# A three-stage decoder kernel: denominator products in rounded halves, table loads as steps of their own, the last feed-forward chunk stacked, and a new order of all steps

## Time and profile before

| | us |
|---|---|
| median of three runs | 876.79 |
| lowest and highest | 876.32, 876.93 |
| the profiled execution | 872.71 |
| its span, first to last instruction | 870.9 |
| a round of the loop | 49.9 |
| PE busy in the span | 824.3 (95%) |
| DVE busy | 698.4 (80%) |
| ACT busy | 587.0 (67%) |
| POOL busy | 262.5 (30%) |
| granted clock, mean | 0.999 |

### The profile page before, as it was taken

How to read it: one execution, slowest core, us unless ns; L and a number is a source line. 1 busy time by engine, 2 the same in 40 slices (tenths; PEclk the granted TensorE clock), 3 DMA queues, 4 the chain that set the end, 5 groups by cost and what they waited for, 6 DMA issues and landing times. The chain is left out here.

```text
span 870.9 us, 21260 instructions
## 1 busy us (share of the span) xinstructions
PE 824.3 (95%) x7296; PEld 699.3 (80%) x7296; DVE 698.4 (80%) x1673; ACT 587.0 (67%) x1527; POOL 262.5 (30%) x443
## 2 busy tenths in 40 slices
PE   9888999999899999999999999999999999998986
PEld 5667788888788888888888888888888888876764
DVE  6889789796979879797988979798897979785643
ACT  5465478785776777686776868676786768674632
POOL 0304223333323333332332233332232333222231
PEclk9999999999999999999999999999999999999999
DMA  8231201111020111111011111111111111101010
GB/s 292 78 101 36 64 14 43 50 50 56 36 62 16 42 48 48 54 41 61 13 41 60 36 54 48 54 36 34 44 39 51 48 54 37 56 2 44 13 55 7
DMA packets 31223, 44.03 MB, mean 51 GB/s; under 512 B 2512, under 2 KB 23120, under 8 KB 31184
## 3 DMA queue, kind: packets, MB, share of 16 engines
q1 hardware_dynamic: 27696, 32.94, 11.4%
q0 software_dynamic: 2048, 6.30, 2.4%
q10 hardware_dynamic: 1440, 4.28, 1.6%
HBM read 28.81 MB, written 14.70 MB: 50 GB/s over the span
## 5 line engine op out<-in xcount | busy, mean ns | idle before, releaser
L681 ACT ACTIVATE prob<-bank,b_folded 128x256 f32<-128x256 f32 x128 | 53.6, 470 | 97.8 <-PE bank L1125 96.8
L872 DVE TENSOR_TENSOR a_s<-bank,const 128x512 f32<-128x512 f32 x112 | 71.2, 682 | 47.4 <-PE bank L1229 26.5
L718 ACT ACTIVATE w_raw_or_stage_c<-bank,c_nmax 128x128 f32<-128x128 f32 x256 | 90.4, 402 | 15.3 <-DVE c_nmax L1038 15.3
L718 ACT ACTIVATION_READ_ACCUMULATOR w_raw_or_stage_c<-bank,c_nmax 128x1 f32 x256 | 62.1, 243 | 0.0
L785 DVE TENSOR_TENSOR b_s_lo<-prob,b_s_hi 128x512 fp32r<-128x512 f32 x64 | 45.3, 708 | 8.2 <-ACT b_s_hi L565 8.2
L443 POOL TENSOR_TENSOR f_rs<-f_mv,const 128x2 f32<-128x2 f32 x32 | 6.1, 191 | 147.5 <-DVE f_mv L794 147.5
L1038 DVE TENSOR_REDUCE c_nmax<-bank 128x4 f32<-128x512 f32 x64 | 40.5, 676 | 11.6 <-PE bank L1409 11.6
L1125 PE MATMUL bank<-b_s_hi,w_mlp_hi 128*128 128x256 f32 x256 | 45.1, 299 | 0.4 <-ACT prob L681 0.3
L1511 PE MATMUL bank<-ones_bf 128*128 128x512 bf16 x160 | 44.4, 396 | 1.0 <-POOL ones_bf L435 1.0
L1420 PE MATMUL bank<-const,w_raw_or_stage_c 128*128 128x128 f32 x256 | 39.6, 278 | 5.5 <-ACT w_raw_or_stage_c L718 4.9
L565 ACT ACTIVATE b_s_hi<-prob 128x512 fp32r<-128x512 f32 x64 | 41.1, 642 | 3.6 <-PE bank L1125 3.0
(11 more groups left out here) (257 smaller groups left out, 2683.7 us busy)
## 6 DMA issues: line engine op xcount, KB each, us to landing
token_rows<-norm_x_rms SPq DMA_DIRECT2D x16, 513.0 KB, 3.8
x_in<-in_x SPq DMA_DIRECT2D x16, 256.0 KB, 3.3
qc<-in_ctx SPq DMA_DIRECT2D x16, 256.0 KB, 2.7
b_f<-in_ctx_t SPq DMA_DIRECT2D x16, 256.0 KB, 3.0
x<-in_x SPq DMA_DIRECT2D x16, 256.0 KB, 2.7
out<-w_raw_or_stage_c SPq DMA_DIRECT2D x16, 256.0 KB, 2.2
w_raw_or_stage_c<-in_w ACTq DMA_DIRECT2D x4, 512.0 KB, 6.3
w_raw_or_stage_c<-in_w_gu ACTq DMA_DIRECT2D x4, 341.0 KB, 3.2
```

The lines of the kernel that those rows point to most:

```text
L681: act_in(prob[:, 2 * (j % 2) + n, :], b0[:, n * T:(n + 1) * T], ACT.Gelu, bias=b1p[:, f:f + 1]).then_inc(b_gelu.sem, 1)
L718: act_in(c_e[g % 2][:, j * R:(j + 1) * R], C_SCORES[g][:, j * R:(j + 1) * R], ACT.Exp, bias=c_nmax[:, n:n + 1], accum_out=c_den[:, head:he ...
L872: tt(heads(A_MASKED[t][n][:, :]), heads(A_SCORES[n][:, :]), tri.unsqueeze(1).broadcast_to([P, 4, P]), ALU.mult).then_inc(a_scput.sem, 1)
```

## The change

Denominator: `a_kq`'s product is split into a high part (new step `a_qhi`, ACT) and a low part (new step `a_qlo`, DVE) in the tiles of `a_tr`, and `a_den` makes four rounded products with the block matrix, which is now kept rounded (`head_block_r`), in place of two plain ones. The block matrix and the row of indices are loaded into a work tile and copied from there.

Last chunk: 682 features fill five chunks of 128 and 42 of the sixth (FL = 42). The 42 are now written three times: the last chunk of the gated values holds the high part, the low part's source and its copy beside each other (two more DVE operations in `c_gate_1`), W3's last chunk holds matching high and low rows, and `c_ff_1` needs one product for it in place of three. `c_gtlo_1` works on two chunks.

Tables: the preload of `a_qout` goes; three steps `b_set_ln`, `b_set_exp` and `b_set_gelu` load the three sets.

Order: all steps stand in a new order, and WEIGHTS_AT and WARM_AT are new (193 filler products in place of 146, besides the 14 at the start).

```diff
+FL = FF % P
+FLAT = FF - FL
...
-a_kout+ c_gu_1++ b_dtp+ b_rtp+ c_tanh_1++ c_gu_2++ b_sid+ b_fput+ b_dput+ b_rput+ b_fmean+ a_ktp+ c_gtlo_1++
-c_gtp_0++ c_gtp_1++ a_vput+ b_kept++ a_sput+ b_fd+ a_den+ c_hsc+ b_fnormed+ a_mask+ b_sexp+ a_dnear+ c_y++
-c_gthi_0++ a_kput+ c_ff_0++ c_gthi_1++ a_state+ a_dinv+ a_rstd+ c_ff_1++ b_hlo+ a_scput_0+ c_ht+ b_htp+
-a_scput_1+ a_scput_2+ a_scput_3+ a_score_0+ a_dput+ a_scput_4+ c_qk+ c_hput+ b_hhi+ b_gelu_0+ b_up_0+ b_fb2++
-a_scput_5+ a_score_1+ c_v+ a_scput_6+ a_scput_7+ a_att_0+ b_rstd+ b_up_1+ b_qb+ c_qkput+ b_glo_0+ a_mean
-a_att_1+ a_y+ b_glo_1+ b_ghi_0+ b_gelu_1+ b_ghi_1+ b_up_2+ a_ylo+ a_normed b_glo_2+ b_orstd++ c_rstd+ c_max_0+
-c_max_1+ b_down_0+ b_up_3+ c_score+ c_max_2+ a_proj+ b_down_1+ a_done+ b_mean c_etp_0+ c_rms1+ c_max_3+ b_glo_3+
-b_down_2+ c_etp_1+ c_vput+ c_etput_0+ b_normed b_down_3+ b_gelu_2+ a_yhi+ c_etput_1+ c_etp_2+ b_ghi_2+ b_gelu_3+
-b_o+ c_h2rms++ c_exp_0+ c_hx++ c_dinv+ c_pick+ c_etp_3+ c_exp_1+ c_etput_2+ b_ghi_3+ c_etput_3+ b_omean+ a_tlo
-c_exp_2+ c_exp_3+ a_tp c_o+ b_tanhk b_onormed+ b_done+ c_mean c_h2put+ c_dtp+ b_pnorm c_dbc+ c_normed c_h2lo+
-b_diff c_rscore a_thi b_frstd+ c_rank c_att+ c_dput+ c_sel b_vq b_v c_idxput c_put++ b_ratio c_keep+ c_gate_0+
-b_tanhq a_phi_q b_vput c_h2sq+ c_ob+ c_xo+ a_phi_k c_h2hi+ a_qout a_q b_log c_gate_1+ a_csum c_h2tp+ a_kq a_k
-c_gu_0+ c_sbc c_tanh_0+ a_val c_gtlo_0+ c_idx
+b_qb+ a_vput+ c_sbc+ b_set_ln b_sexp+ c_gthi_0++ b_orstd++ c_gu_0++ a_kput+ a_qlo+ a_qhi+ b_fput+ c_gtlo_1++
+b_fmean+ a_dnear+ c_idx+ c_gu_1++ a_sput+ a_mask+ c_gthi_1++ a_dput+ c_rstd+ c_y++ b_dtp+ c_hput+ b_fnormed+
+b_set_exp c_rms1+ a_scput_0+ a_scput_1+ b_rtp+ b_hlo+ c_gu_2++ a_scput_2+ a_scput_3+ b_sid+ a_ktp+ b_hhi+
+a_scput_4+ a_dinv+ b_glo_0+ a_scput_5+ a_scput_6+ c_hx++ c_h2rms++ a_scput_7+ b_gelu_0+ c_gtp_0++ a_mean a_y+
+b_ghi_0+ b_fd+ b_gelu_1+ c_qkput+ c_pick+ a_ylo+ c_gtp_1++ b_glo_1+ a_den+ c_ff_0++ b_gelu_2+ a_normed b_glo_2+
+c_ht+ a_state+ c_ff_1++ b_frstd+ b_ghi_1+ c_max_0+ c_max_1+ a_score_0+ b_htp+ c_max_2+ c_vput+ c_qk+ a_yhi+
+a_done+ b_ghi_2+ b_up_0+ b_gelu_3+ c_exp_0+ b_mean c_put++ c_max_3+ b_glo_3+ c_exp_1+ a_score_1+ c_etput_0+
+b_normed c_v+ a_att_0+ b_up_1+ c_etput_1+ b_ghi_3+ b_fb2+ c_exp_2+ c_exp_3+ a_att_1+ b_o+ b_up_2+ b_down_0+
+c_dinv+ a_thi c_etput_2+ b_up_3+ c_dbc+ c_score+ a_proj+ c_etput_3+ c_ob+ b_down_1+ c_etp_0+ b_set_gelu++
+c_dput+ b_tanhk b_down_2+ b_omean+ c_etp_1+ b_kept+ b_down_3+ a_tlo c_etp_2+ c_o+ a_tp c_etp_3+ b_onormed+
+b_tanhq b_done+ c_dtp+ a_rstd c_h2put+ c_keep+ c_att+ c_h2sq+ c_xo+ c_mean a_qout b_pnorm c_normed c_rscore
+b_diff c_h2lo+ a_q c_rank c_sel b_vq a_phi_q c_idxput a_kout b_ratio c_h2hi+ b_vput c_h2tp+ b_log c_tanh_0+
+a_phi_k c_tanh_1+ a_k c_gate_0+ b_v a_csum a_val b_rstd a_kq c_gate_1+ b_dput b_rput c_gtlo_0+ c_hsc
...
-                if not first(b):
-                    nc.scalar.preload_act_table_set("natural_log_exp_and_others")
...
+            def a_qhi_(b):
+                act_e.wait_ge(*a_kq(b))
+                act_e.wait_ge(*a_qk(b))
+                act_e.wait_ge(*a_val(b))
+                copy(flat(a_tr[0][:, :, :]), a_e0[:, :], a_qhi)
+
+            def table(name):
+                def step(b):
+                    nc.scalar.preload_act_table_set(name)
+                return step
...
+                    if n == len(loads) - 1:
+                        last = [w[:, FFP // P - 1, :] for w in w3]
+                        dve.wait_ge(raw_lo.sem, n + 1)
+                        ts(last[0], last[0].bitcast(F32), C["w3_high"], None, ALU.mult).then_inc(w3_last.sem, 1)
+                        dve.wait_ge(w3_last.sem, 1)
+                        stt(last[0], last[1].bitcast(F32), C["w3_low"], last[0].bitcast(F32), ALU.mult, ALU.add) \
+                            .then_inc(w3_last.sem, 1)
...
+            def a_qlo_(b):
+                dve.wait_ge(*a_qhi(b))
+                low(flat(a_tr[1][:, :, :]), a_e0[:, :], flat(a_tr[0][:, :, :]), a_qlo)
...
+                    if j:
+                        high, lowp = act[:, FF + FL:FF + 2 * FL], act[:, FF:FF + FL]
+                        stt(high.bitcast(F32R), half[:, n - FL:n], c_r2q[:, 0:1], up_bank[:, n - FL:n], ALU.mult, ALU.mult) \
+                            .then_inc(c_gate.sem, 1)
+                        dve.wait_ge(*c_gate(b, 5))
+                        tt(lowp, act[:, FLAT:FF], high, ALU.subtract).then_inc(c_gate.sem, 1)
...
+                    n = 3 - j
+                    low(flat(act_t[1][:, 3 * j:3 * j + n, :]), G_BANK[j][:, 0:n * P],
+                        flat(act_t[0][:, 3 * j:3 * j + n, :]), c_gtlo)
...
-                    pe.wait_ge(const_rest.sem, 16)
-                    pe.wait_ge(v_zero.sem, 11)
-                pe.wait_ge(*a_kq(b))
+                    pe.wait_ge(v_zero.sem, 12)
                 pe.wait_ge(*a_vput(b))
-                for c in range(DC):
-                    last = mm(a0[:, c * T:(c + 1) * T], C["head_block"], a_e0[:, c * T:(c + 1) * T], start=True, stop=True)
+                for part, ready in ((0, a_qhi), (1, a_qlo)):
+                    pe.wait_ge(*ready(b))
+                    for c in range(DC):
+                        last = mm(a0[:, c * T:(c + 1) * T], head_block_r[:, :], a_tr[part][:, c, :], start=part == 0 and c == 0,
+                                  stop=part == 1, skip_group_check=True)
...
-                    pe.wait_ge(*c_gate(b, 2 * j + 2))
+                    pe.wait_ge(*c_gate(b, (2, 6)[j]))
...
-                        for k in range(3 * j, 3 * j + 3):
+                        for k in range(3 * j, 3 * j + (3 if a == 0 else 3 - j)):
                             last = mm(c1[:, 0:D], act_t[p][:, k, :], w3[q][:, k, :], start=j == 0 and a == 0 and k == 0,
-                                      stop=j == 1 and a == 2 and k == 5, skip_group_check=True)
+                                      stop=j == 1 and a == 2 and k == 4, skip_group_check=True)
...
+    for n in (1, 2):
+        w3[:, FLAT + n * FL:FLAT + (n + 1) * FL] = a["L0_ffn_W3"][:, FLAT:]
```

44 lines of the change are left out of this document (26 added, 18 removed).

## The result

The changed kernel takes 879.51 us (median of 16 runs, 877.04 to 889.25), the kernel before 876.24 us beside it (16 runs, 873.38 to 879.43). The ratio is 1.0046, with a 95% interval of 1.0028 to 1.0064: slower, by 2.5 to 5.6 us. The forecast of 897.5 missed, and so did its range. The profiled execution took 881.06 us (span 879.2), before 872.71 (span 870.9). So the two traces lie 8.35 us apart and the medians 3.3: the trace before is of an execution quicker than all sixteen of those runs, and a difference between two traces is not yet one between two kernels. Medians are of all executions; a ratio leaves out those over 1.5% above the fastest of their kernel (two of `fold_fill`), and it can differ from the quotient of the medians by 0.3%.

A forecast was written before the change was run, and what follows sets the result against it. Before, a round (49.9 us) was as long as PE's instructions; in the new order a chain of 18.5+8.2+13.9+10.95 = 51.5 bounds it. +1.6 over 13 rounds, 20.8, on the median 876.8 gave 897.5 us, range 881 to 909.

The forecast's parts named there:

- The sum of the chain, 51.5: Waits and engine order around one loop round, added up as a floor: 51.5 us against 49.9, +1.6 a round.
- Head and tail I leave at 0, within 3 either way: First and last rounds, outside the loop: no change in time, within 3 us either way.
- The difference does not depend on which: Base of the forecast: the difference was added to the median, 876.8 us, and not to the profiled execution, 872.7.
- A: Second attention product to c_xo, through ACT and DVE, with PE standing 1.1 us for c_o: 18.5 us.
- B: c_xo to the rank, with b_v moved in at 1.83 us and a back edge of 0.40: 8.2 us.
- C: c_rank to the first score, with a_qlo and small operations added to a dense DVE: 13.9 us, 13.82 before.
- D: First score to the second attention product: 10.95 us, between 10.2 without a POOL and a_dinv meeting and 11.3.
- stands as a_ylo stood, until 7.9: a_dinv on DVE, held by POOL's b_kept until 7.9 us after the score; a_scput_5 then starts 0.75 late.
- rival 2: Short chain: POOL and a_dinv miss each other, small operations take 0.05; round 50.45, 884 us. Chance 0.12.
- Every link has a measured duration: Argument against PE staying the bound, a case that needed operations to answer sooner by 1.6 us a round.
- rival 1: PE stays the bound of the loop because A and C are shorter than placed; faster, 861 us. Chance 0.13.
- rival 4: A table switch stops ACT for another load's 1.28 us beyond its row; round 52.8, 914.5 us. Chance 0.01.

The follow-up runs named there:

- fold_fill: Changed kernel with three 512-column fillers ahead of a_ktp of batch 0, between PE's two runs of one-column products: 884.29 us, 1.0086 to the kernel before.
- ends2: ends with the ninth and tenth weight steps moved behind the fourth scput of batch 1: 876.64 us, 1.0006 to the kernel before.
- hsc_later: Changed kernel with c_hsc behind c_gtlo_1 on VectorE in all rounds: 880.75 us, 1.0078 to the kernel before.
- ends: fold_later2 with b_glo_1 ahead of a_ylo, and c_hsc behind c_gtlo_1 only in the rounds after the loop: 875.87 us, 1.0023 to the kernel before.
- fold_later2: Changed kernel with PE's second run of one-column products behind a_score_0 and six fillers before a_den: 878.22 us, 1.0071 to the kernel before.
- fold_later: Changed kernel, five fillers ahead of a_den, PE's second one-column run meant for behind a_score_0 but issued at 16.19: 880.45 us, 1.0103 to the kernel before.
- glo1_first: Changed kernel with one swap on VectorE, b_glo_1 ahead of a_ylo: 879.63 us, 1.0046 to the kernel before.
- weights_moved: Changed kernel with three of the thirteen weight steps, all in the first rounds, moved to later places: 883.03 us, 1.0099 to the kernel before.
- combined: Changed kernel with the edits of glo1_first, weights_moved and hsc_later together: 882.65 us, 1.0092 to the kernel before.
- glo1_att: glo1_first with c_dput ahead of b_set_gelu on ScalarE and c_o ahead of a_tlo on VectorE: 883.56 us, 1.0098 to the kernel before.
- bv_back: Changed kernel with b_v back between c_att and c_xo on PE: 886.15 us, 1.0125 to the kernel before.
- order_only: Changed kernel's order, table steps, fillers and weight placement with the old arithmetic: 886.21 us, 1.0125 to the kernel before.

## Why the prediction was wrong, by its own steps

Three steps failed. **The sum of the chain, 51.5**, is why the forecast was too high: the round is 49.84. **"Head and tail I leave at 0, within 3 either way"** is why the kernel is slower all the same: the loop gains in the traces, and the ends lose 5.7 and 4.4 us. **"The difference does not depend on which"**, the median added to in place of the trace, made the forecast 5.6 us higher still.

**The ends.** I never laid the new order against the first and the last rounds, where one engine has nothing else to do while it waits.

- Head, +5.7 us. 1.9 of it lies ahead of the first `a_y`, where traces of the same code differ by as much, and 3.8 behind it (49.25 us to the first `b_o`, for 45.42 in the one trace before), in every trace with that code. The first `a_y`, before and after:

```profile
31.41 0.69 DVE L879 SCALAR_TENSOR_TENSOR a_norm<-bank,a_e 128x512 f32<-128x512 f32 x1 [0.21 <-PE bank L1247]
```

```profile
33.28 0.69 DVE L908 SCALAR_TENSOR_TENSOR a_norm<-bank,a_e 128x512 f32<-128x512 f32 x1 [0.21 <-PE bank L1284]
```

I looked for the cause in the low parts of weights, which stand in VectorE's queue ahead of what PE needs:

```profile
42.32 0.93 DVE L796 SCALAR_TENSOR_TENSOR w_ffn_gu_lo<-w_raw_or_stage_c,vectors_by_column,w_ffn_gu_hi 128x682 fp32r<-128x682 f32 x1 [1.13 <-ACT w_ffn_gu_hi L571]
```

With the wait it keeps `b_pnorm` from starting for 2.0 us; others of 2.03 and 0.92 us (57.95 and 62.71) stand ahead of `b_fnormed` and `b_hlo`. `ends2` moved the last two and gained 0.0, so they don't cost what they take; for the first it is argued only. A rival that no run tested is the filler products, which I had also counted at 0. The stretch holds 41 of them for 30, 10.22 us for 7.84 (windows of the filler's line alone, before and after; first the column of PE):

```profile
31.41:76.83 45.42, 7.84 (x30) 2.57 (x28) 1.00 0.20 57
```

```profile
33.28:82.53 49.25, 10.22 (x41) 3.73 (x40) 1.00 0.18 53
```

And 2.6 of the 3.8 us are lost between the second batch's `a_dnear` and its `a_y` (57.01 to 72.82, before 54.65 to 67.90), where 17 fillers stand for 5, 4.07 us for 1.60.

- Tail, +4.4 us. In the last round `c_hsc` waits for the gathered rows, and `c_gtlo_1`, ready long before, stands behind it on VectorE; the product with W3 waits for that. VectorE, then PE:

```profile
844.09 0.35 DVE L1062 TENSOR_SCALAR c_rden_or_products<-picked_rows 128x256 f32<-128x256 f32 x1 [3.90 <-DMA picked_rows<-token_rows,row_of_slot]
```

```profile
844.92 0.41 PE L1412 MATMUL bank<-const,c_rden_or_products 128*128 128x128 f32 x2 [2.20 <-DVE gated_t_lo L809]
```

After that wait the clock is at 0.57 between 845 and 849. With `c_hsc` behind (`hsc_later`, `ends`) the tail is 3.8 and 3.9 us shorter, but that is not what the edit is worth: the tail of `fold_later2`, which has the code of the changed kernel there, is 3.5 shorter too (last `b_o` at 822.60).

```profile
840.43 0.35 DVE L1063 TENSOR_SCALAR c_rden_or_products<-picked_rows 128x256 f32<-128x256 f32 x1 [1.96 <-DMA picked_rows<-token_rows,row_of_slot]
...
868.51 0.42 DVE L1129 TENSOR_TENSOR w_raw_or_stage_c<-bank,w_raw_or_stage_c 128x256 f32<-128x256 f32 x1 [0.97 <-PE bank L1543]
```

The last gather took 5.1 us from issue to landing in the trace of the changed kernel, 3.5 in this one and before. Some traces with the changed kernel's arithmetic beside the one before, in us from the last `b_o`:

| trace | `c_hsc` of the last batch | last `c_y` |
|---|---|---|
| before | 17.61 | 45.05 |
| `fold_later`, `fold_later2` | 17.63, 17.83 | 45.73, 45.91 |
| `glo1_first`, `weights_moved` | 19.05, 19.49 | 47.16, 47.60 |
| changed kernel | 19.74 | 49.44 |
| `c_hsc` behind: `ends`, `hsc_later`, `combined` | 17.74, 17.90, 19.14 | 45.48, 45.63, 46.88 |

Read down the table: a landing that is later by 1.7 us makes the tail longer by 1.7, and the fall of the clock, which only the changed kernel's trace and `glo1_att`'s have there, adds some 1.6. At an equal landing the new order costs 0.7 us, and the place of `c_hsc` about half of that. So of the 4.4 us 2.1 are the late landing, 1.6 the clock and 0.7 the kernel's own; why the gather lands late in some executions stays open. With the head's 3.8, this 0.7 and the loop's gain of 0.8 to 1.7, the kernel's own loss is 2.8 to 3.7 us, an estimate from the traces, and the medians have 3.3.

**The chain**, measured in the round above:

| term | forecast | measured | why |
|---|---|---|---|
| A, attention to `c_xo` | 18.5 | 18.50 (614.12 to 632.62) | right number, wrong reason |
| B, `c_xo` to the rank | 8.2 | 7.75 (to 640.37) | back edge of 0.40 gone, `b_v` 1.53 and not 1.83 |
| C, rank to score | 13.9 | 13.48 (to 653.85) | gaps I had put in did not open |
| D, score to attention | 10.95 | 10.12 (604.00 to 614.12) | no meeting of POOL and `a_dinv` |

D is the largest error: "stands as a_ylo stood, until 7.9". I took the gap of 1.64 us that POOL had behind the row put for fixed. It was `c_keep`'s: by the code that step waits for `y_stored`, the landing of the put, which came 2.5 us after its issue in the trace before. With `c_keep` moved away, `b_fb2` follows the put without a gap (605.19 + 1.04, then 606.26), and `b_kept` is over in time. That is the mechanism of rival 2, to which I gave 0.12; it left me at 884, since the rest of the chain was too long also. B and C counted each instruction at the length of its row where starts lie closer together. In A, the forecast named ACT and VectorE as the floor, but PE's own products filled it to `c_dtp`: `glo1_first` removed gelu_3's wait and the stretch kept its 26 us. "Every link has a measured duration", my argument against rival 1, says nothing of which chain is the longer. 13 rounds at 1.66 too many make 21.6 us. Trace against trace the forecast was 12.4 too high (872.7 + 20.8 against 881.06): 21.6 for the chain, less 10.1 for the ends, plus 0.9 that the fifteen rounds between the `b_o` gained beyond 13 x 0.06. The other 5.6 of the 18.0 (897.5 to 879.51) come from the third step: the trace before lay 4.1 under the median that I added to, the trace after 1.5 above its own. The whole change is known from 32 runs (2.5 to 5.6 us slower), its parts only from single traces.

**Right** were these steps: eight loads in a round and almost no idle time before them (0.9 us before the 48 own ones, 1283 ns each), so that rival 4's price doesn't show. The Trainium skill, "ScalarE: Activation LUTs", section "What ACT_TABLE_LOAD costs", has 2.66 us for a switch to another set, drain included; the trace doesn't agree, since an exponential starts at 622.64, 1.29 us after the load at 621.35. Right were also `a_yhi` behind gelu_2, VectorE idle 2.25 before `a_ylo`, `a_ylo` at 0.69, `c_xo` waiting 0.95 for `c_o` (I had 1.1), `c_gu_2` waiting for `c_gate_0` (0.41, I had 0.7), the score waiting for VectorE, and `a_den`'s four products at 0.56 from start to start (I had 0.50), and the small operations at 0.25 and 0.20. That the kernel would be slower came true by luck, for reasons that I hadn't given.

**Not foreseen**: the falls of the clock. The one in the head costs 0.7 us in the changed kernel's trace. In the loop they come in some executions and not in others; `fold_fill`'s runs took 876.69 and 877.03 us at a mean clock of 0.999 and 886.92 and 889.34 at 0.986 and 0.983. Why a given execution has them and another none stays open; `bv_back`, without the wait before `c_xo`, had none in its loop rounds but one at 798.

Open also: what the fillers and the first weight step cost in the head, and whether some order of the ends would beat the kernel before.

## What to carry to other kernels

Price the first and the last rounds of a pipelined order by themselves: a step that is covered in the steady round can be bare there (the swap of `glo1_first` gained 0.27 us a round and lost 2.0 in the head). Before crediting an edit with a shorter stretch, look at the same stretch in a trace whose code there is unchanged: the tail was 49.4 us in one and 45.9 in another. In a round that several engines fill, ask for each stretch which one is continuously busy in it before shortening another's chain: the wait of 0.95 us ahead of `c_xo`, which stands ahead of VectorE's row, gave nothing when it was filled. And put a table load before the wait of its first user, in a place where ACT is free: here two loads a round more on ACT made the round 2.46 us shorter.

## What the runs showed of the hardware that I had not expected

- With PE recorded as busy almost without a break, two runs of sixteen one-column products among its work, the granted clock fell to half in 13 traces of 14 (0.50 between 20 and 22 us in the changed kernel's). It stayed at 1.00 in the three with the second run moved and more fillers, but also in `order_only`, so the cause isn't isolated.
- In a loop where PE is 95% busy, two waits of 0.5 and 0.95 us within 3 us are followed in some rounds, not in most, by a stretch at 1.2 GHz, 1.35 us of the round each.
- A gap on an engine may belong to the step behind it and not to the one before: POOL's 1.64 us after the row put, which the profile puts down to "issue", went with `c_keep`, which waits for the put's landing.
- The same gather took 3.5 us to land in one execution and 5.1 in another, and a tail that waits for it moved with it.
